# Experts scatter weighted rows into token order, and the delta rule's gates move into the experts' stage

## The reference

```python
# layer 2: mixture of experts: 8 experts, 2 for each token, and a shared one
scores = softmax(layernorm(x) @ gate_w.T)        # the two largest of scores + gate_b are taken
y = x + shared(h) + sum over the 2 chosen e of scores[e] * expert_e(h)   # h = layernorm(x)
# expert: hidden = swiglu((h @ w1 + b1) * (h @ w3 + b3)); out = hidden @ w2 + b2
# layer 3: gated delta rule, its gates for each token and head (8 heads):
h = layernorm(y)
beta  = sigmoid(h @ Wb) * 2.0
alpha = exp(-exp(A_log) * softplus(h @ Wa + dt_bias))
state = alpha * (state - beta * retained * k) + beta * v * k
```

## Time and profile before

| | us |
|---|---|
| median of 3 runs (4054.55 to 4061.96) | 4057.43 |
| the profiled execution | 4019.23 |
| its span | 4017.4 |
| mean granted TensorE clock in it | 0.844 of full |
| busy: PE, DVE, ACT, POOL | 3306.8, 2361.9, 1368.9, 152.0 |

### The profile page before, as it was taken

How to read it: one execution, slowest core, us unless ns; L and a number is a source line. 1 busy time by engine, 2 the same in 40 slices (tenths; PEclk the granted TensorE clock), 3 DMA queues, 4 the chain that set the end, 5 groups by cost and what they waited for, 6 DMA issues and landing times. The chain is left out here.

```text
span 4017.4 us, 53883 instructions
## 1 busy us (share of the span) xinstructions
PE 3306.8 (82%) x18986; PEld 2568.6 (64%) x18986; DVE 2361.9 (59%) x6068; ACT 1368.9 (34%) x2745; POOL 152.0 (4%) x149
## 2 busy tenths in 40 slices
PE   6999958888999999033698989898989889578777
PEld 3665534456999999022486868677676779455454
DVE  5555235545777777354668676766768584344442
ACT  2323212222444444000444453535344443022232
POOL 0000000023000000600000000000000000000000
PEclk8999969998999999555788889797979796578787
DMA  1000040024898987411201011010110100100000
GB/s 59 21 16 11 11 149 11 11 86 178 320 319 321 320 319 274 133 44 52 72 33 33 33 33 35 30 38 28 41 46 19 54 16 7 51 11 11 22 17 11
DMA packets 200529, 331.11 MB, mean 82 GB/s; under 512 B 29665, under 2 KB 154618, under 8 KB 199106
## 3 DMA queue, kind: packets, MB, share of 16 engines
q1 hardware_dynamic: 194114, 310.80, 22.3%
q0 software_dynamic: 6144, 16.79, 1.3%
HBM read 279.17 MB, written 48.37 MB: 82 GB/s over the span
## 5 line engine op out<-in xcount | busy, mean ns | idle before, releaser
L719 PE MATMUL ex_ps<-ex_xbT,ex_w 128*128 128x128 f32 x4544 | 532.4, 276 | 0.5 <-issue 0.5
L719 PEld LDWEIGHTS ex_ps<-ex_xbT,ex_w 128*128 128x128 f32 x4544 | 526.0, 193 | 4.5 <-issue 0.9
L1355 PE MATMUL de_ps<-de_hT,de_w 128*128 128x512 f32 x640 | 307.6, 639 | 26.4 <-DMA de_w<-in_w_kqv_dram 12.6
L799 ACT ACTIVATE ex_t<-ex_ps,ex_b 128x128 f32<-128x128 f32 x568 | 208.9, 368 | 336.5 <-PE ex_ps L719 320.0
L1355 PEld LDWEIGHTS de_ps<-de_hT,de_w 128*128 128x128 f32 x640 | 129.5, 207 | 187.7 <-issue 185.7
L663 PE MATMUL ex_ps<-ex_xT,ex_w 128*128 128x512 f32 x512 | 231.0, 607 | 14.6 <-DVE ex_gl L876 11.4
L876 DVE SCALAR_TENSOR_TENSOR ex_gl<-ex_ps,ex_b,ex_t 128x128 f32<-128x128 f32 (+1 forms) x316 | 123.6, 391 | 142.4 <-ACT ex_t L799 76.7
L663 PEld LDWEIGHTS ex_ps<-ex_xT,ex_w 128*128 128x128 f32 x512 | 97.6, 194 | 133.4 <-issue 113.6
L1712 DVE SCALAR_TENSOR_TENSOR de_ya<-de_kx,de_taps,de_ya 128x512 f32<-128x512 f32 x192 | 142.4, 750 | 49.8 <-ACT de_ya L1551 45.2
L876 DVE SCALAR_TENSOR_TENSOR ex_gm<-ex_ps,ex_b,ex_t 128x128 f32<-128x128 f32 (+1 forms) x316 | 121.7, 385 | 58.1 <-ACT ex_t L772 44.6
L180 PE MATMUL mx_ps<-mx_hT,mx_w_in 128*128 128x512 f32 x320 | 143.2, 604 | 8.3 <-ACT mx_hT L267 8.3
(11 more groups left out here) (382 smaller groups left out, 6368.2 us busy)
## 6 DMA issues: line engine op xcount, KB each, us to landing
ex_w<-in_w_all_dram SPq DMA_DIRECT2D x144, 1024.0 KB, 7.1
ex_w<-in_w_all_dram SPq DMA_DIRECT2D x72, 512.0 KB, 7.9
de_w<-in_w_kqv_dram SPq DMA_DIRECT2D x80, 256.0 KB, 2.8
de_ab<-alpha_d SPq DMA_DIRECT2D x8, 2048.0 KB, 8.4
ex_xs_d<-ex_yb SPq DMA_DIRECT2D x71, 128.0 KB, 1.9
ex_xb<-ex_xs_d SPq DMA_DIRECT2D x71, 128.0 KB, 7.3
ex_ys_d<-ex_yb SPq DMA_DIRECT2D x71, 128.0 KB, 7.3
mx_xin<-in_x_dram SPq DMA_DIRECT2D x8, 512.0 KB, 3.9
```

The source lines that it names most:

```text
L719: m = pe.matmul(ps[:, n % 4, x * BLK:(x + 1) * BLK], w[:, k, part * HID + c * P:part * HID + (c + 1) * P], xbT[sx][:, k, :], start=(k == 0 ...
L799: act.activation(t1[:, n % 2, 0:BLK], ps[:, n % 4, 0:BLK], ACT.Identity, bias=b13[s][:, 0, n:n + 1]).then_inc(t1_ready, 1)
L1355: m = pe.matmul(ps[:, n % 2, :], w[:, g % SLOTS, k, n % 2 * P:(n % 2 + 1) * P], hT[:, k, :], start=(k == 0), stop=(k == KT - 1))
```

## The change

- `xs_d` rows grow from 256 to 258 floats: the 256 features, the weight of the expert (column 256) and a destination row (column 257, an integer). `h` and `xb` grow with them. The zeros are now stored as rows of 257 floats from a tile `blank`, and column 257 of all 9088 rows is stored by one further DMA of single elements from the new constant `dest`, behind the zeros and ahead of the loads of the third and later batches. Its value names a spare row for the padding rows.
- The scatter into `xs_d` goes choice by choice: 32 DMAs of first choices; then POOL waits for all of them, rewrites columns 256 and 257 of `h` with two small copies, and issues 32 of second choices.
- In the block loop DVE multiplies the result by the row's weight as it leaves PSUM (in place of the copy), and POOL scatters `yb` by the destination column of `xb` into `y2_d`, where rows 0 to 4095 are the tokens' first choices in token order, 4096 to 8191 the second, and the rest spare. SP's store goes. SP's load of the rows of block j+3 now stands behind the weights of block j+3 and waits for the scatter of block j, since that scatter reads its addresses from the same `xb` slot.
- After the loop SP loads each batch's two halves of `y2_d` with two plain DMAs (into the weight slots), three batches ahead, and DVE adds them to `acc` with two instructions of 128x1024 for each batch. POOL's gathers are gone.
- `stage_gates` is gone. Its work follows inside `stage_experts` from `acc` in place: the norm for two batches at once (`norm_two`), transposes and copies by batch, gate columns by batch into 32 partitions each, so that four batches (a half) fill 128 partitions; the small DVE chain once for each half with 128x128 in place of 128x32 for each batch; the running products on 32x512 for each half. Eight batches of norms and transposes are interleaved with the adds, the first half's gates with the last two batches'. Five constants more are loaded at the stage's start, and PE and DVE wait for all 13.

The diff, cut to its core:

```diff
-        xs_d = nc.dram_tensor("ex_xs_d", (ROWS, DIM), F32, kind="Internal").ap()
-        ys_d = nc.dram_tensor("ex_ys_d", (ROWS, DIM), F32, kind="Internal").ap()
+        xs_d = nc.dram_tensor("ex_xs_d", (ROWS, RW), F32, kind="Internal").ap()
+        y2_d = nc.dram_tensor("ex_y2_d", (PAIRS_ALL + ROWS, DIM), F32, kind="Internal").ap()
...
             for n in range(NB):
-                sp.dma_start(xs_d[n * BLK:(n + 1) * BLK, :].rearrange("(t p) d -> p t d", p=P), yb[0][:, :, :]).then_inc(zeroed, 16)
+                sp.dma_start(xs_d[n * BLK:(n + 1) * BLK, 0:DEST], blank[:, :]).then_inc(zeroed, 16)
+            sp.wait_ge(c_loaded, 16 * N_CONST)
+            sp.dma_start(xs_d[:, DEST:DEST + 1].rearrange("(n p) c -> p n c", p=P), dest[:, 2 * NT:2 * NT + NB].bitcast(F32).unsqueeze(2),
+                         allow_slow_non_contiguous=True).then_inc(zeroed, 16)
...
-            def store_block(j, s):
-                sp.wait_ge(yb_ready, j + 1)
-                sp.dma_start(rows(ys_d, j), yb[s][:, :, :]).then_inc(y_stored[s], 16)
-
-            for j in range(NB):
-                if j + SLOTS < NB:
-                    sp.wait_ge(xbTp, j + 1)
-                    sp.dma_start(xb[j % SLOTS][:, :, :], rows(xs_d, j + SLOTS)).then_inc(xb_loaded[j % SLOTS], 16)
-                    sp.wait_ge(down_ready, BATCH + j + 1)
-                    load_block(j + SLOTS, j % SLOTS)
-                store_block(j, j % 2)
+            for j in range(NB - SLOTS):
+                sp.wait_ge(down_ready, BATCH + j + 1)
+                load_block(j + SLOTS, j % SLOTS)
+                sp.wait_ge(y_stored[j % 2], 16 * (j // 2 + 1))
+                sp.dma_start(xb[j % SLOTS][:, :, :], rows(xs_d, j + SLOTS)).then_inc(xb_loaded[j % SLOTS], 16)
...
+            for j in range(NB):
+                pool.wait_ge(xb_loaded[j % SLOTS], 16 * (j // SLOTS + 1))
+                pool.wait_ge(yb_ready, j + 1)
+                pool.indirect_dma_start(y2_d, bass.IndirectOffsetOnAxis(xb[j % SLOTS][:, 0, DEST:DEST + 1].bitcast(U32), 0),
+                                        yb[j % 2][:, 0, :], None).then_inc(y_stored[j % 2], 16)
...
-                dve.tensor_copy(yb[sx][:, :, :], ps[:, 4 + sx, 0:BT * DIM].rearrange("p (t d) -> p t d", d=DIM)).then_inc(yb_ready, 1)
+                dve.tensor_scalar(yb[sx][:, 0, :], ps[:, 4 + sx, 0:DIM], xb[j % SLOTS][:, 0, WEIGHT:WEIGHT + 1], None, ALU.mult).then_inc(yb_ready, 1)
...
+            for i in range(3):
+                add_pairs(2 * i), add_pairs(2 * i + 1), norm_two(i)
+            raw_gates(0)
+            add_pairs(6), add_pairs(7)
+            decays(0)
+            norm_two(3)
+            products(0), turned_products(0)
+            raw_gates(1), decays(1), products(1), turned_products(1)
```

More of the change, by code:

```diff
@@ L449, in stage_experts @@
     SLOTS = 3
+    H, HB, GW = D_HEADS, BATCH // 2, 32
+    TH = TT * HB
+    LN_TERMS = 8
     ctx = ExitStack()
@@ L603, in _ @@
             pool.wait_ge(pos_ready, 1)
             pool.wait_ge(h_ready, BATCH)
[L605 to L615 removed]
+            pool.wait_ge(ext_set, 2)
@@ new lines, in _, with add_pairs, norm_two @@
+            norm2 = Chain(dve, s5, 2 * 2 * TT + 12)
+            gates = Chain(dve, s6, 23)
+            def add_pairs(b):
+                dve.wait_ge(y_loaded[b % SLOTS], 32 * (b // SLOTS + 1))
+                to = acc[:, b * TT:(b + 1) * TT, :]
+                for r in range(2):
+                    dve.tensor_tensor(to, to, w1[b % SLOTS][:, r, :].rearrange("p (t d) -> p t d", d=DIM), ALU.add).then_inc(added, 1)
+                    dve.wait_ge(added, 2 * b + r + 1)
+            def norm_two(i):
+                norm2.start(i)
+                t0 = 2 * TT * i
+                for t in range(2 * TT):
+                    norm2(dve.bn_stats(stats2[:, t, :], acc[:, t0 + t, :]), wait=(t == 2 * TT - 1))
+                dve.memset(pace[:, :], 0.0)
+                for t in range(2 * TT):
+                    norm2(dve.bn_aggr(mv2[:, t, :], stats2[:, t, :]), wait=(t == 2 * TT - 1))
+                norm2(dve.tensor_scalar(vv2[:, :], mv2[:, :, 1], LN_EPS, None, ALU.add))
+                norm2(rsqrt(dve, norm2, rstd2[:, :], vv2[:, :], tmp2[:, :]))
+                for t in range(2 * TT):
+                    m = dve.tensor_scalar(h[:, t0 + t, 0:DIM], acc[:, t0 + t, :], mv2[:, t, 0:1], rstd2[:, t:t + 1], ALU.subtract, ALU.mult)
+                m.then_inc(hd_ready, 1)
+                norm2.end()
@@ new lines, in _, with raw_gates @@
+            spread = lambda tile: tile[:, :].unsqueeze(1).broadcast_to([P, TH, H])
+            by_batch = lambda v: v.rearrange("p (t b) h -> p b t h", b=HB)
+            def raw_gates(half):
+                gates.start(half)
+                dve.wait_ge(prTp, half + 1)
+                pre = ps[:, 6 + half, :].rearrange("p (a x) -> p a x", x=GW)
+                gates(dve.tensor_tensor(pa[:, :, :], pre[:, :, 0:H], spread(dt_bias), ALU.add))
+                gates(dve.tensor_scalar(zb[:, :, :], pre[:, :, H:2 * H], -80.0, None, ALU.max))
+                dve.scalar_tensor_tensor(out=aa[:, :, :], in0=pa[:, :, :], scalar=-1.0, in1=pa[:, :, :], op0=ALU.mult,
+                                         op1=ALU.max).then_inc(aa_ready, 1)
@@ new lines, in products @@
+            def products(half):
+                dve.wait_ge(arow_ready, half + 1)
+                if half:
+                    dve.wait_ge(gamTp, half)
+                gates(dve.tensor_tensor(az[:, half, :], arow, keep[:, :], ALU.mult))
+                gates(dve.tensor_tensor(first, arow, az[:, half, :], ALU.subtract))
+                gates(dve.tensor_tensor_scan(gam, arow, first, 1.0, ALU.mult, ALU.max))
+                dve.tensor_copy(gend[:, half, :], gam.rearrange("h (c s) -> h c s", s=D_CHUNK)[:, :, D_CHUNK - 1]).then_inc(gam_ready, 1)
@@ new lines, in turned_products @@
+            def turned_products(half):
+                dve.wait_ge(gamTp, half + 1)
+                dve.tensor_copy(bg[:, half, :, 1, :, :], by_batch(ps[:, 6 + half, 0:TT * GW].rearrange("p (a h) -> p a h", h=H))).then_inc(bg_ready, 1)
+                gates.end()
+            for i in range(3):
[5 more added lines that the diff above has]
+            products(0), turned_products(0)
```

380 lines of the change are left out of this document (179 added, 201 removed).

## The result

| | before | changed |
|---|---|---|
| median of 4 runs, us | 4058.51 (4054.55 to 4061.96) | 3909.72 (3897.38 to 3913.38) |
| ratio, 95% interval | | 0.9628 [0.9605, 0.9651] |
| the profiled execution, us | 4019.23 | 3913.38 |
| its span, clock | 4017.4, 0.844 | 3911.5, 0.860 |

The page's busy line after, the answer to the earlier trace rows: PE has 16 us less work, DVE 52 less (the gathered adds and the small chains of 128x32), POOL 6 more.

What follows compares the result with a forecast made beforehand. Bound by short steps waiting on each other after the loop, by PE within it. Terms -186.5 + 2.5 + 9.4 + 4.0 + 7 = -163.6 us gave 3856, carried over to 3893.8; range 3865 to 3965.

Steps and rivals of the forecast that it cites:

- The tail: Last block's copy to delta's first DMA: 107.5 us in place of 294.0, gain 186.5 (bounds 175 and 195).
- Ahead of the first scatter: Before the first scatter: five constants 2.5 us, column 257's DMA 9.4 (5 to 42), POOL's later start 1.5.
- SP's issue bounded them before, so 0, at most 8: Zeros' stores with rows of 1028 bytes at odd offsets: 0 us added, at most 8.
- The scatter's split: Scatter into `xs_d`: wait for the 32nd landing 1.2 us, two copies 0.7, hop 0.6; PE's first-row wait 15.
- The loop: Block loop: rows land 11.8 us after the w2 matmuls' end, against 11.6, costing 7 (bounds 0 and 31).
- stall = (L - 11.6)/2: Block loop: PE's stall, 68 times; L is the rows' landing after the w2 matmuls' end D, taken as 11.8 us.
- rival 1: Block loop: the rows' load becomes the bound, L = 15, stall 1.7 us, 116 in all, time some 4003; chance 0.12.
- The carrying over: Whole kernel: 3856 us on the profiled execution, plus the 38 by which before's median exceeded that execution, 3893.8.
- the prediction's last sign: Delta stage: the forecast is wrong if it changes by more than a few us, as the change touches nothing there.
- 3 (slower): Block loop: scatter and load delayed by each other's queue, L = 18, 218 us, time 4105; decides from 16.4; chance 0.05.
- 2 (element DMA at 42, zeros slower by 8): Before the first scatter: element DMA 42 us or more, unaligned zeros' rows 8 more, time 3935; chance 0.13.
- 4: Tail and block loop: tail hides better (clock, overlap), L below 11.6, time 3875 us; chance 0.15.

Runs made afterwards that it cites:

- Experiment 2: Kernel before with only the gates made inside the experts' stage, block-order stores and POOL's gathers kept: 3915.92 us, ratio 0.965 to before.
- experiment 3: Changed kernel up to the adds, scatter into token order, but gates in a stage of their own as before: 4046.71 us, ratio 0.997 to before.
- experiment 4: Changed kernel with column 257's element DMA issued behind the fourth batch's input load instead of ahead of the third's: 3857.67 us, ratio 0.9598 to before.
- experiments 4 to 6: Changed kernel with the late element DMA (3857.67 us), with a fourth slot for the rows (3858.37), with both (3843.70); before took 4019.86.
- experiment 5: Changed kernel with a fourth slot for a block's rows, loaded ahead of the weights: 3858.37 us, ratio 0.9602 to before.
- experiment 8: One session: changed kernel again 3897.8 us; with fourth slot, zeros spread behind input loads and element DMA last 3857.34; with POOL waiting after every eighth scatter 3881.4.

## Why the prediction was right, step by step

**The tail: right, the sum and its parts.** From the last product to delta's first DMA: 105.8 us, forecast 107.5; saved 188.2, forecast 186.5. The start of the tail, then its four marks, in the timeline of the changed kernel:

```profile
1686.19 0.48 DVE L1125 TENSOR_SCALAR ex_yb<-ex_ps,ex_xb 128x256 f32<-128x256 f32 x1 [2.09 <-PE ex_ps L793]
1687.43 0.95 POOL L676 DMA_INDIRECT ex_y_d<-ex_yb,ex_xb  x1 [7.26 <-DVE ex_yb L1125]
1689.86 9.29 SPq L627 DMA_DIRECT2D ex_w<-ex_y_d  x8
1695.73 2.49 DVE L1142 TENSOR_TENSOR ex_acc<-ex_acc,ex_w 128x1024 f32<-128x1024 f32 x2 [9.05 <-DMA ex_w<-ex_y_d]
```

```profile
1736.59 0.28 DVE L1167 TENSOR_TENSOR ex_pa<-ex_ps,ex_dt_bias 128x128 f32<-128x128 f32 x1
...
1746.11 0.23 DVE L1174 TENSOR_SCALAR ex_ln<-ex_ea 128x128 f32<-128x128 f32 x1 [3.68 <-ACT ex_eb L939]
...
1759.16 2.67 DVE L1156 TENSOR_SCALAR ex_h<-ex_acc,ex_mv,ex_rstd 128x256 f32<-128x256 f32 x8
...
1788.63 0.40 SPq L636 DMA_DIRECT2D bg_d<-ex_bg  x1
...
1792.02 0.37 SPq L1326 DMA_DIRECT2D de_ident<-in_ident_dram  x1
```

Copy to first adds 9.5 (forecast 3.0 + 5.5); adds and three norms to the first gate operation 40.9 (42.7); from there to the end of the last norm, 1761.83, 25.2 (22.3); from there to the barrier's other side 30.2 (32.7). The row at 1746.11 explains the third: DVE waits 3.7 us for ACT's exponential, because ACT first copies a batch that PE turns before it. I had named no wait there. The last part is shorter since PE's clock rose, which the prediction had as its other case (13 shrinks to 10). Behind the last norm PE turns and multiplies batch 6 in 6.3 us at a granted clock of 0.53 (the level of 1.2 GHz for almost all of it; PE works 5.2 us of them), then batch 7 in 4.1 us at 1.00 (2.4 GHz), so 10.4 in place of 13. The parts miss by 1.0, -1.8, 2.9 and -2.5 us, with both signs, so that the whole came out nearer than they did; that much is luck. Experiment 2 adds what the sum didn't say: of 188 us some 140 come with the gates made inside the stage, and the other 49 with the scatter in place of the gathers (experiment 3).

**Ahead of the first scatter: right in kind, too small.** Forecast 2.5 + 9.4 + 1.5 = 13.4, measured 20.2 (19.9 to 20.5 in three profiles). The wait for the third batch's input is now

```profile
DVE ex_stats L972 <- DMA ex_xin<-x_d: 29.2, 1, 29.2
```

against 8.3 and a forecast of 18. The constants cost less than the 2.5 forecast: DVE's wait for the last of them grew from 6.7 to between 8.1 and 8.2. The element DMA's landing in the second profile of the changed kernel:

```profile
L592 SPq DMA_DIRECT2D ex_xs_d<-ex_dest x1: 747/747/747, 565.7 to 565.7; - x1
...
DMA to landing us min/median/max: 19.4/19.4/19.4
```

In the first profile it is 18.1, in the third 19.3. Divided by the 568 elements for each engine that is 32 to 34 ns each, or 27 by the 15.1 us it took in experiment 4, where I had 16.5 from small packets of another kind; the upper bound of 74 was far off. So its size was twice what I took, but on the path it cost only 9 to 12 us, near the 9.4: "its whole time is on the path" was wrong, and the two errors cancel by luck. The step that failed in the sum is the other one, "SP's issue bounded them before, so 0, at most 8": the zeros. With rows of 1028 bytes the DMA engines and no longer SP's issue are the limit (share 0.85 to 1.10, 291 to 260 GB/s), a store lands after 8.1 us in place of 1.9, and the load behind them in the same queue waits too. With the element DMA out of the way the wait for the third batch is still 10 us longer than before, and the first scatter, constants included, 9 us later. The Trainium skill (page DMA: Bandwidth & Descriptors, How a descriptor splits into AXI transactions) says of reads that one that doesn't begin on a multiple of 256 bytes fetches bytes that it doesn't use. It speaks of reads alone, and what lies at odd offsets here is what the stores write: no run shows that this is the reason, or separates the rows' alignment from their length. Its rule on transfers below 512 bytes, which the prediction weighed toward the upper end of 42 us, names no price; 18.1 to 19.4 lies between the 9.4 and the 42, nearer the lower.

**The scatter's split: right.** Forecast 2.5 behind the first scatter, measured 1.1 to 2.0 in the three profiles of experiments 4 to 6, where nothing stands still, and 14.8 to 15.6 of PE's wait where I announced 15.

**The loop: right mechanism, too small.** Forecast +7, measured +22.5, +13.1 and +17.5 in the three profiles, with blocks 9.3 to 9.4 us apart in place of 9.1. PE's waits for rows in 530 us of the loop of the first:

```profile
PEld ex_ps L769 <- DMA ex_xb<-ex_xs_d: 19.1, 34, 1.2
...
PE ex_ps L769 <- DMA ex_xb<-ex_xs_d: 11.9, 23, 1.0
```

By the prediction's own formula, stall = (L - 11.6)/2 in 68 blocks, L was 12.0 to 12.3 and not 11.8. The landing of POOL's scatters had been guessed well, 5.4 to 7.1:

```profile
DMA to landing us min/median/max: 2.4/6.9/8.6
```

Two other steps were short. I took POOL's issue at 0.6 us behind the matmuls' end D; the rows at 1686.19 and 1687.43 have 1.24 from the start of DVE's multiplication, which takes 0.48 of it, and POOL needs another 0.76. One block in the loop, with D at 1102.59:

```profile
1100.70 1.89 PE L793 MATMUL ex_ps<-ex_w,ex_hid 128*128 128x256 f32 x8
1102.63 0.48 DVE L1125 TENSOR_SCALAR ex_yb<-ex_ps,ex_xb 128x256 f32<-128x256 f32 x1 [0.43 <-PE ex_ps L793]
1103.87 0.96 POOL L676 DMA_INDIRECT ex_y_d<-ex_yb,ex_xb  x1 [8.13 <-DVE ex_yb L1125]
1110.88 0.34 SPq L622 DMA_DIRECT2D ex_xb<-ex_xs_d  x1
1115.39 0.44 PE L769 MATMUL ex_ps<-ex_ident,ex_xb 128*128 128x128 f32 x2 [0.84 <-DMA ex_xb<-ex_xs_d]
```

POOL issues at D + 1.3 and SP's load goes out at D + 8.3, just what I had called the latest; in the loops of the three profiles its median is D + 8.2. The rows then come 4.5 us later here, and 2.9 to 6.9, mostly near 4, in the blocks where PE waits for them; rival 1 had written 3 for this leg. So L is set by the scatter's chain, together with what the weights ahead still add to its last leg. Which of the two steps weighs more no run tells; experiment 5 shows that all of it went through the rows' load.

**The carrying over.** "The median is 38 us above that execution; carried over" stood without a reason, and that it held is luck: between the two profiles of before the second stretch grew by 40.2 us, while first transposes to first product took 2.3 less, so the 38 us were the standstill, and both kernels have it in a session that has it. Terms by their measured sizes, -188.2 + 20.2 + 1.1 + 17.7 (the mean of three), make -149.2, against -148.8, -155.2 and -159.4 in three comparisons of medians. The two profiles that come from one session, both with the standstill, give -189.6 + 21.0 + 1.6 + 12.1 = -154.9, against -155.2 there. All fall short of the forecast of -163.6, chiefly by what the zeros and the loop cost beyond it. The delta stage and what follows changed by 4 us at most, as the prediction's last sign asked.

**The rivals.** 1 (loop at 4003) and 3 (slower) fell: L stayed far from 15. The turning point of 3 was off by a little: a gain of 163.6 already holds the loop's 7, so it is L = 16.6 and not 16.4. 2 (element DMA at 42, zeros slower by 8) was half right: its second half came true, its first did not. 4 fell, since the tail hid little more than forecast and L was above 11.6.

## What to carry to other kernels

Before two profiles are subtracted, each is held against the timings of its own kernel, and both are cut at the same points; a stretch that grew without a cause in the change is looked for in a second profile of the old kernel. A DMA that nobody waits for can still cost much of its length, if it stands in a queue ahead of a load that is waited for (here the first scatter came 9 to 12 us earlier for one moved line, and 25.7 earlier with the zeros moved too). And a new step in a loop's DMA chain is sized with the copy in it, from the end of the matmuls to the issue on the other engine, 1.3 us here, and is best taken off the chain with one more buffer.

## What the runs showed of the hardware

Beside POOL's 64 scatters, PE, DVE and ACT can stand still, at a cost of some 40 us, while the profile names no instruction or DMA that DVE and ACT wait for (releaser "remote" or "issue"). It shows in both kernels and in parts of the change, in two sessions of four, by the times of before in every run of such a session (4050 to 4066 us against 4008 to 4025), and one chip had sessions of both kinds. Matmuls that still run in it come singly, one in 2.8 us, here in the kernel of experiment 2:

```profile
925.52 1.01 PE L709 MATMUL ex_ps<-ex_xT,ex_w 128*128 128x512 f32 x1 [1.79 <-issue]
...
928.32 1.01 PE L709 MATMUL ex_ps<-ex_xT,ex_w 128*128 128x512 f32 x1 [1.79 <-issue]
...
931.12 1.01 PE L709 MATMUL ex_ps<-ex_xT,ex_w 128*128 128x512 f32 x1 [1.79 <-issue]
```

It is over within 10 us of POOL's last scatter; in the third profile of the changed kernel PE works for a few us in between, from 953.1, and stops again. In the second profile of before the last scatter starts at 951.0, and the first instructions of DVE and ACT behind the gap are

```profile
958.88 1.22 DVE L905 TENSOR_TENSOR ex_acc<-ex_acc,ex_ps 128x1024 f32<-128x1024 f32 x1 [63.34 <-remote]
```

```profile
960.36 1.26 ACT L772 ACTIVATE ex_t<-ex_ps,ex_b 128x512 f32<-128x512 f32 x2 [67.01 <-remote]
```

Gaps of 2 us in POOL's issue, one after eight scatters, end it too (experiment 8); the single gap in the changed kernel, after 32, did not.

One guess is that the engines lack their next instructions. Queues between 905 and 980 us, in the second profile of before, then in the first (packets, MB, share of 16 engines):

```profile
q0 software_dynamic: 1827, 4.98, 18.5%
q1 hardware_dynamic: 288, 0.26, 1.2%
```

```profile
q1 hardware_dynamic: 2341, 5.25, 19.3%
q0 software_dynamic: 1854, 5.04, 18.8%
q8 instruction: 2, 0.03, 0.2%
q14 instruction: 1, 0.01, 0.0%
```

With the standstill the queues q8 and q14, which the profile labels "instruction", have no row. But this can as well follow from the standstill as cause it: engines that stand still use no instructions up. And in the same profile there is no such packet from 903 to 985 us, although DVE, ACT and PE start again at 958.9 to 961.9. So the packets don't support the guess; what holds the engines back beside POOL's scatters, and what makes a session one kind or the other, is open.
